# Moving G's mix beside K's and V's, and two matmul groups ahead of the shared expert's first chunk, in an attention-and-experts kernel

## The reference

```python
delta = shifted - h
x1 = jnp.tanh(jnp.tanh((h + delta * x_proj_mu) @ xl_w1.T) @ xl_w2.T + xl_b2).reshape(B_, T_, 5, R)
mus = jnp.einsum('btnr,hnr->btnh', x1, x_out_w.reshape(H_, 5, R)) + x_bias
r, k, v, g = ((h + delta * mu) @ w.T for mu, w in ...)
w = jnp.tanh((h + delta * w_mu) @ w_w1.T) @ w_w2.T + w_b
wd = jnp.exp(-jnp.exp(w))
def step(S, xs):
    r_t, k_t, v_t, w_t = xs
    o_t = einsum('bhk,bhkv->bhv', r_t, S) + sum(r_t * bonus * k_t) * v_t
    S = S * w_t[..., None] + k_t[..., None] * v_t[..., None, :]
    return (S, o_t)
x = _layernorm(x + (groupnorm(o) * silu(g)) @ o_w.T)
out = _layernorm(x + shared_expert(x) + sum over the top 2 of 16 experts of weight * expert(x))
```

## Time and profile before

| what | value |
|---|---|
| median of 3 runs | 841.86 us (839.3 to 841.96) |
| the profiled execution | 840.05 us, of which 838.2 us are the span |
| PE busy | 773.3 us (92%) |
| DVE, ACT, POOL busy | 532.9, 479.6, 545.6 us |
| granted PE clock, mean over the span | 0.986 |

### The profile page before, as it was taken

One profiled execution on the slowest core, in us unless ns is written; L12 is line 12 of the kernel. 1 busy time (PEld: TensorE's weight loads), 2 busy tenths in 40 slices (PEclk: granted clock), 3 DMA queues, 4 the chain that ended last, 5 costly groups with the idle time before them and its releaser, 6 DMA issues.

```text
span 838.2 us, 27821 instructions
## 1 busy us (share of the span) xinstructions
PE 773.3 (92%) x8906; PEld 588.8 (70%) x8907; DVE 532.9 (64%) x1714; ACT 479.6 (57%) x1250; POOL 545.6 (65%) x678
## 2 busy tenths in 40 slices
PE   9999999999999999999977759999999999999994
PEld 6666656665566655665555439999999999989741
DVE  4548797777877787678764525555555555555366
ACT  3456666666566655665554305655665665656456
POOL 5565688888888888788886642455554555545444
PEclk9999999999999999999999989999999999999998
DMA  5001111221122202220114512222222222221094
GB/s 175 14 29 43 46 50 38 56 69 49 34 60 65 63 25 60 62 61 26 47 37 128 184 50 72 77 72 62 70 64 61 72 63 60 68 59 44 21 403 189
DMA packets 48271, 61.40 MB, mean 73 GB/s; under 512 B 8594, under 2 KB 33432, under 8 KB 48048
## 3 DMA queue, kind: packets, MB, share of 16 engines
q1 hardware_dynamic: 39200, 42.83, 17.3%
q0 software_dynamic: 8704, 17.06, 6.0%
q10 hardware_dynamic: 272, 0.26, 0.1%
HBM read 37.73 MB, written 23.43 MB: 73 GB/s over the span
## 4 chain that ended last, share of the span: by engine, by line
PE 68%; POOL 13%; issue 9%; ACT 3%; DVE 3%; another core or an unknown queue 2%; SPq 1%; DMA 0%; POOLq 0%; ACTq 0%; DVEq 0%
PE psB L630 16%; PE psO L642 15%; PE psO L559 5%; POOL w_ring L1001 5%; PE psP L342 5%; POOL dispatched_rows L1021 4%; PE psB L501 3%; PE psO L347 2%; PE psP L423 2%; PE psB L491 2%; PE psB L479 2%; PE psP L429 2%; PE psP L619 2%; PE psP L333 2%
## 5 line engine op out<-in xcount | busy, mean ns | idle before, releaser
L1044 POOL DMA_INDIRECT expert_results<-yw_all,row_tail x144 | 147.7, 1026 | 151.8 <-ACT yw_all L914 120.5
L904 ACT ACTIVATE hide<-psB,w_ring 128x128 f32<-128x128 f32 x432 | 126.7, 365 | 85.0 <-DVE hide L1375 44.1
L1021 POOL DMA_INDIRECT dispatched_rows<-rows,slot x128 | 131.0, 1023 | 35.6 <-issue 31.4
L630 PE MATMUL psB<-x1T,w_ring 128*128 128x128 f32 x1152 | 142.3, 277 | 5.2 <-issue 4.6
L642 PE MATMUL psO<-w_sb,hide 128*128 x1152 | 142.6, 277 | 0.5 <-ACT hide L904 0.4
L630 PEld LDWEIGHTS psB<-x1T,w_ring 128*128 128x128 f32 x1152 | 134.2, 192 | 8.6 <-issue 7.9
L642 PEld LDWEIGHTS psO<-w_sb,hide 128*128 128x128 f32 x1152 | 134.2, 192 | 1.0 <-issue 0.9
L1001 POOL TENSOR_TENSOR w_ring<-w_ring,tot 128x128 f32<-128x128 f32 (+2 forms) x160 | 117.6, 754 | 0.0
L1365 DVE COPY w_ring<-w_sb 128x516 f32 x144 | 56.5, 434 | 81.2 <-issue 81.2
L1096 DVE SCALAR_TENSOR_TENSOR psP<-psP,cols,delta 128x512 f32<-128x512 f32 x80 | 57.3, 753 | 54.5 <-PE psP L342 54.5
L863 ACT ACTIVATE hide<-psO,cols 128x512 f32<-128x512 f32 x64 | 44.1, 689 | 62.8 <-PE psO L559 59.3
(11 more groups left out here) (204 smaller groups left out, 1381.4 us busy)
## 6 DMA issues: line engine op xcount, KB each, us to landing
rows<-dispatched_rows SPq DMA_DIRECT2D x144, 66.0 KB
w_sb<-expert_results SPq DMA_DIRECT2D x5, 1024.0 KB, 10.5
h_res<-in_hidden SPq DMA_DIRECT2D x16, 256.0 KB, 3.0
out<-w_sb SPq DMA_DIRECT2D x16, 256.0 KB, 3.4
hT<-in_hidden_t SPq DMA_DIRECT2D x15, 256.0 KB, 4.0
w_sb<-in_w SPq DMA_DIRECT2D x14, 256.0 KB
expert_results<-yw_all,row_tail POOLq DMA_INDIRECT x144
w_sb<-in_w SPq DMA_DIRECT2D x2, 1032.0 KB
```

The lines of the kernel that those rows point to most:

```text
L630: last = mm(up_ps(p)[:, c // 2, at:at + PART], w1b[w][s][:, c * 128:(c + 1) * 128], xTe[p][:, s * PART:(s + 1) * PART], start=True, stop=True)
L904: last = A(hide[p][:, c, s * PART:(s + 1) * PART], psB[:, 2 * p + c // 2, at:at + PART], ACT.Relu, bias=w1b[w][s][:, HIDDEN + c:HIDDEN + c ...
L1021: G.indirect_dma_start(rows_dram[:, :], bass.IndirectOffsetOnAxis(slot[u % 2][:, j, k:k + 1], 0), rows[k][u % 2][:, j, :], None).then_inc( ...
L1044: G.indirect_dma_start(back_dram[:, :], bass.IndirectOffsetOnAxis(row_tail[:, i, s, 1:2].bitcast(u32), 0), yw[i][:, s, :], None, bounds_ch ...
```

## The change

It does three things. G's mix is written to bank 0 of psB and follows K's and V's at once, after a wait for the copy of that bank to `k_tok`. On PE, `b_k_tok` now stands ahead of `b_o_near`, and both, the three mixes and `b_kv` stand ahead of `f_up 0`; `f_up 1` takes the place that G's mix had between `a_k` and `a_v`. On ACT, the relu `f_hid 0` moves behind the copies of `k_tok`, the chunk decay and R_near; `f_hid 1` moves behind K and K_near, and stands ahead of `a_decay`; the copy `c_rows1` moves behind `a_decay`. DVE and POOL keep their order.

```diff
-MIX_BANK = {MIX_W: 0, MIX_R: 1, MIX_K: 0, MIX_V: 1, MIX_G: 1}
...
+        mix_ps = {MIX_W: P0, MIX_R: P1, MIX_K: P0, MIX_V: P1, MIX_G: psB[:, 0, :]}
...
-            def a_mix_k_v(u):
+            def a_mix_k_v_g(u):
                 done(pe, "exp_w", u)
                 done(pe, "r_done", u)
                 pe.nop(nofuse=True)
-                mix(P0, MIX_K)
-                mix(P1, MIX_V)
+                mix(MIX_K)
+                mix(MIX_V)
+                before(pe, "k_tok", u)
+                mix(MIX_G)
...
-            def a_mix_g(u):
-                done(pe, f"mixed{MIX_V}", u)
-                mix(P1, MIX_G)
...
             def body(at):
+                at(2, b_k_tok)
+                at(2, b_o_near)
+                at(3, fill, 5)
+                at(3, a_mix_k_v_g)
+                at(2, b_kv)
                 at(0, f_up, 0)
-                at(2, b_o_near)
-                at(2, b_k_tok)
-                at(3, fill, 5)
-                at(3, a_mix_k_v)
-                at(2, b_kv)
-                at(0, f_up, 1)
                 at(0, c_place)
                 at(3, fill, 10, 5, 5)
                 at(3, a_k)
-                at(3, a_mix_g)
+                at(0, f_up, 1)
                 at(3, a_v)
                 at(0, f_up, 2)
...
                 at(2, a_w)
-                at(-1, f_hid, 0)
                 at(1, b_k_tok)
                 at(1, b_chunk_decay)
                 at(2, a_r_near)
+                at(-1, f_hid, 0)
+                at(2, a_k)
+                at(2, a_k_near)
                 at(-1, f_hid, 1)
-                at(2, a_k)
+                at(2, a_decay)
                 at(-1, c_rows1)
-                at(2, a_k_near)
-                at(2, a_decay)
                 at(-1, c_top_exp)
...
-                ps = unflat(psP[MIX_BANK[n]])
+                ps = unflat(mix_ps[n])
```

More of the change, by code:

```diff
@@ L334, in by_seq, with mix @@
                 return i
-            def mix(ps, n):
+            def mix(n):
                 if n < 4:
@@ L341, in mix @@
                 kw = {"tile_position": (96, 0)} if n == 3 else {}
-                mm(ps, w, a, start=True, stop=True, **kw).then_inc(sem(f"mix_ps{n}"))
+                mm(mix_ps[n], w, a, start=True, stop=True, **kw).then_inc(sem(f"mix_ps{n}"))
             def fill(u, *n):
@@ L383, in a_mix_w_r @@
                 pe.nop(nofuse=True)
-                mix(P0, MIX_W)
-                mix(P1, MIX_R)
+                mix(MIX_W)
+                mix(MIX_R)
             def a_decay_hid(u):
@@ L1106, in a_add @@
                 dve.nop(nofuse=True)
-                V.tensor_tensor(mixed[MIX_BUF[n]][:, :, :], unflat(psP[MIX_BANK[n]]), hT[u % 2][:, :, 1:T + 1], ALU.add).then_inc(sem(f"mixed{n}"))
+                V.tensor_tensor(mixed[MIX_BUF[n]][:, :, :], unflat(mix_ps[n]), hT[u % 2][:, :, 1:T + 1], ALU.add).then_inc(sem(f"mixed{n}"))
             def a_gate(u):
```

## The result

The changed kernel takes **889.44 us** (median of 4 runs, 887.25 to 892.28), against 841.91 us (839.3 to 845.22) for the kernel before beside it: a ratio of 1.0575, with a 95% interval of 1.0555 to 1.0595. The profiled execution took 887.25 us, of which 885.4 us are the span. The forecast was 850, with a range of 842 to 859: the direction was right, the size not.

The account below looks back on a forecast made before the run. PE, busy for 92% of the span, was taken to bound the kernel, with POOL close behind. 13 rounds at 0.7 us (9.1), +0.9 for three earlier rounds and 0 for the last gave +10 on 840.05: 850, range 842 to 859.

Parts of the forecast that it names:

- The wait ahead of the transposes: On PE ahead of `b_k_tok`: with nothing covering POOL's step 4 any more, PE stands still for 1.35 us.
- G's mix at nothing: On PE beside K's and V's mixes: a third group of rows was taken to cost 0 us.
- The mixes and `b_kv` 0.4 us later: On PE behind the transposes: the mixes, and DVE's work on K, `b_kv` and `a_k` with them, come 0.4 us later.
- K's copy comes at 252.67 + 0.4 = 253.07: On ACT behind K's projection: the copy starts only 0.4 us later than before, so `a_v` is 0.4 us late.
- if its result is as late as the second chunk's is now (0.83): On ACT behind `f_up 0`: its relu was assumed to start 0.83 us after the matmul's end, at 251.6.
- the upper bound of 1.1: Per full round, for POOL's step 1: at most 1.1 us later, if all signals are late and hold `f_up 2`.
- `a_decay` behind the relu, and POOL: On ACT and POOL: `a_decay` ends at 255.15 to 255.4, delaying POOL's step 0; this side alone gives 0 to 0.3 us.
- The falling clock: Rival, in the rounds: new PE waits bring 5 more clock falls at 1.6 us each, 858 us; chance 0.15.
- The last rounds "at 0, with 1 us either way": The last rounds, which have no K step, were set at 0 us of change, with 1 us either way.
- "The signals are prompt": Rival, in the full rounds: PE's results come without delay, each round is 0.3 us shorter, 837 us; chance 0.14.

Follow-up runs that it names:

- g_only: The kernel before with G's mix alone moved, right behind K's and V's mixes: 822.81 us, ratio 1.0004, on a chip with prompt results.
- late_after: The changed kernel with added ACT copies, 2.2 us ahead of K's copy and 1.1 us ahead of the first relu: 871.0 us, ratio 1.0584.
- after_fill2: The changed kernel with five dummy matmuls in PE's wait ahead of the transposes, on a chip with late results: 880.11 us, ratio 1.0323.
- tail_old: The changed kernel with the old order of `f_up 0`, `f_up 1` and their relus in the three last rounds alone: 823.89 us, ratio 1.0024.
- chunk_back2: The changed kernel with `f_up 0` and its relu back in their old places, on a chip with late results: 885.16 us, ratio 1.0438.

## Why the prediction was wrong

**The wait ahead of the transposes: right.** 1.35 us forecast, 1.35 and 1.36 found, released by POOL's step 4.

**G's mix at nothing: right.** Six records in 1.13 us, against 1.06 in the chain for the pair. The estimate from the Trainium skill (TensorE: Matmul & The Clock Gate, Part 3) of up to 0.3 us for a third group is not borne out by this row. g_only can't tell, as G's mix waits for `k_tok` there.

**The mixes and `b_kv` 0.4 us later: right, and the heart of what came.** The depth of `b_kv` went from 0.20 to 0.55. The prediction wrote this 0.4 into the sum as 0.4.

**"K's copy comes at 252.67 + 0.4 = 253.07": wrong.** This is the step that failed. It carried K's lateness of 1.24 us over as a property of the place, as "if its result is as late as the second chunk's is now (0.83)" did for `f_up 0`, and the upper bound of 1.1 ("all late, and `f_up 2` held by them") rested on the same sizes. Measured at 0.55 us depth were 2.32 us from K's projection to its copy and 1.27 us from `f_up 0` to its relu, and up to 2.4 us for `f_up 0`'s signal in the rounds behind a fall. Counted from the start of level 4 (243.78 before, 230.81 after), the steps behind K's copy are later with it:

| step | forecast later by | measured later by |
|---|---|---|
| K's copy | 0.4 | 1.42 |
| `a_v` | 0.4 | 1.42 |
| `f_up 2` | 0.7 to 0.9 | 1.64 |
| POOL's step 1 | 0.7 | 1.74 |

So the whole 1.74 us of a full-clock round lies in the stretch that the forecast worked out, with its waits in the places that it named, and 1.0 of it is the term that was too small. That K's lateness passes on one to one is what the stretches of late_after and of the first trace show.

**`a_decay` behind the relu, and POOL: mixed.** POOL's wait is there (2.21 and 4.10 us instead of 0.24), but it comes from K's late copy. To put `a_decay` first made the full-clock rounds longer both times (26.57 against 26.31, 29.53 against 29.22). I had named its place as a price; it is none.

**The falling clock: a rival that belonged into the forecast.** It was given 5 falls, at 1.6 us each, and a chance of 0.15. There were 10 more in the rounds, at 1.5 us, 15 of the 35.4 us there. The price was right, the count bounded by nothing. I had argued that in all other rounds the clock held, but the longest wait on PE in those rounds was 0.67 us, and the new ones are 1.35, 1.04, 0.66 and up to 2.3. Which of them brings the clock down stays open: the one trace of after_fill2 shows that filling the wait of 1.35 us was not enough. The Trainium skill (same page, Part 1) calls the full clock the exception, to be earned by a busy array; the traces agree in the direction, 37.5 us at half clock where PE is busy for 25.4 of 29.2 us, and 3.4 where it is busy for 26.1 of 27.5 (on a prompt chip none in the rounds of the changed kernel, at 24.7 of 26.3).

**The last rounds "at 0, with 1 us either way": wrong.** They took 10.3 us more here and 7.9 on a prompt chip, where tail_old gives 6.5 us back. There is no K step there to fill the gap, `f_up 1` no longer covers DVE's `seen` (2.32 us instead of 0.23, in each of the last two rounds), and half-clock time rises from 13.7 to 44.7 us in that stretch.

**"The signals are prompt" would be faster: wrong too.** Where they are prompt, the rounds stay at 26.31 us: POOL's loop is full, and PE's chain with the wait of 1.36 us is as long. The drain makes the kernel slower all the same.

## What to carry to other kernels

A result that comes late in a trace is not a constant to carry along with the operation: look at how its lateness changes with its place against the DMAs beside it, and price a move into them at the worst row seen in such a burst, not at the row of the place it leaves. Behind a burst of POOL's indirect DMAs, a few tenths of a microsecond of shift can cost microseconds per round; let the results on which others wait end ahead of it. And count the drain of a pipeline by its own waits, since steps that were hidden in full rounds stand bare there.

## What the runs showed of the hardware that was not expected

- The same kernel takes 822 us on four chips and 842 to 848 on three, and the traces differ in when PE's results are signalled beside POOL's indirect DMAs: 0.04 us after the matmul's end on the former, 1.08 us on the latter, at the same place. Why the chips differ stays open; the DMAs themselves last as long on both (0.95 to 1.3 us).
- Rounds and falls of the clock lock: in chunk_back2 and after_fill2 nearly every round has one and is 30.7 us long, in the changed kernel nearly every second round has two, and such a pair is 61.5 us long.
- Three groups of 32 rows at 512 columns ran in 1.13 us, where one takes 1.12 (L342 in the timeline of g_only), to two PSUM tiles.
